# Token shift by transfers inside SBUF, and one over the sums spread by VectorE, in the transformer gate of a one-core kernel

## The reference, cut to what matters

```python
def shift_token(t):
    t1, t2 = jnp.split(t, 2, axis=-1)
    t2 = jnp.pad(t2, ((0, 0), (1, 0), (0, 0)))[:, :-1]
    return jnp.concatenate([t1, t2], axis=-1)

def _layer(x, wqkv, qs, ksc, wo, lg, lb, w1, b1, w2, b2):
    q, k, v = jnp.split(shift_token(x) @ wqkv, 3, axis=-1)   # to heads
    q, k = rotary_xpos(l2norm(q) * qs, l2norm(k) * ksc)
    o = local_attention(q, k, v)            # softmax over 64 + 64 keys
    x = x + o @ wo
    h = shift_token(x)
    mu, var = h.mean(-1, keepdims=True), h.var(-1, keepdims=True)
    h = (h - mu) / jnp.sqrt(var + 1e-05) * lg + lb
    a, g = jnp.split(h @ w1 + b1, 2, axis=-1)
    return x + (a * jax.nn.gelu(g, approximate=False)) @ w2 + b2
```

## Time and profile before

| | |
|---|---|
| median of 3 runs | 5196.27 us (5194.27 to 5201.23) |
| profiled execution, its own time | 5186.17 us |
| its span | 5184.8 us |
| busy over the span | PE 88%, DVE 61%, ACT 48%, POOL 45% |
| the gate, from the first transfer of a table to the last product | 1158.7 to some 1638 us, 9% of the span |
| steady units | 5 with 20 windows, 1257.71 to 1537.56 us: 56.0 us each |
| outside them | 12 windows of the first unit and the last two |
| one product of 128x512 on PE | two passes, 0.43 us each |
| masks and scores of one window on PE | from 1394.59 to 1396.14 us |

### The profile page before, as it was taken

One profiled execution on the slowest core, in us unless ns is written; L12 is line 12 of the kernel. 1 busy time (PEld: TensorE's weight loads), 2 busy tenths in 40 slices (PEclk: granted clock), 3 DMA queues, 4 the chain that ended last, 5 costly groups with the idle time before them and its releaser, 6 DMA issues. The chain is left out here.

```text
span 5184.8 us, 69828 instructions
## 1 busy us (share of the span) xinstructions
PE 4583.3 (88%) x27948; PEld 2248.3 (43%) x27948; DVE 3137.6 (61%) x4142; ACT 2498.2 (48%) x3813; POOL 2314.1 (45%) x1323
## 2 busy tenths in 40 slices
PE   5999999988987877877799999986799999999997
PEld 3444444445664333333322222223455555555554
DVE  4656565636665777753377777844465655565664
ACT  2344444446664455552256666661244444444443
POOL 0455555558661577780100000000066666666674
PEclk8999999989997899988889999997899999999998
DMA  0000000011110000000000000000000000000000
GB/s 32 3 3 3 3 3 3 3 36 27 32 25 12 2 2 2 1 1 23 3 2 1 2 2 1 1 1 9 10 3 3 3 1 3 3 3 1 3 1 9
DMA packets 57045, 35.95 MB, mean 7 GB/s; under 512 B 31268, under 2 KB 48976, under 8 KB 56464
## 3 DMA queue, kind: packets, MB, share of 16 engines
q1 hardware_dynamic: 56720, 31.49, 2.4%
HBM read 22.16 MB, written 1.05 MB: 4 GB/s over the span
## 5 line engine op out<-in xcount | busy, mean ns | idle before, releaser
L793 DVE TENSOR_REDUCE L_part<-banks 128x2 f32<-128x1024 f32 (+2 forms) x1600 | 1882.0, 1190 | 995.9 <-PE banks L644 856.9
L778 ACT ACTIVATE L_weights<-banks 128x1024 f32<-128x1024 f32 (+1 forms) x1600 | 1580.4, 1000 | 1055.3 <-PE banks L676 841.0
L702 PE MATMUL banks<-L_weights,L_V 128*32 128x512 f32 (+3 forms) x6400 | 1501.6, 605 | 5.8 <-ACT L_weights L778 3.7
L1000 POOL TENSOR_TENSOR L_wsum<-L_wsum,L_weights 128x1024 f32<-128x1024 f32 (+1 forms) x448 | 983.9, 2196 | 55.6 <-ACT L_weights L778 2.8
L983 POOL TENSOR_TENSOR L_wsum<-L_wsum,L_two 128x1024 f32<-128x1024 f32 x240 | 570.4, 2377 | 860.2 <-DVE L_two L967 857.8
L702 PEld LDWEIGHTS banks<-L_weights,L_V 128*64 128x64 f32 (+1 forms) x6400 | 284.7, 123 | 461.5 <-issue 398.5
L676 PE MATMUL banks<-L_QH,L_KH 64*128 64x512 f32 (+3 forms) x1664 | 432.4, 453 | 17.8 <-issue 10.2
L2502 POOL MEMSET F_xr<- 128x16 f32 x1 | 0.1, 125 | 933.8 <-POOLq L97 933.8
L644 PE MATMUL banks<-L_KH,L_QH 64*128 64x512 f32 (+3 forms) x1664 | 373.6, 430 | 30.8 <-ACT L_weights L778 17.5
L676 PE MATMUL banks<-L_QL,L_KH 64*128 64x512 f32 (+3 forms) x1664 | 372.8, 383 | 0.0
L676 PE MATMUL banks<-L_QM,L_onesrow 64*128 64x512 f32 (+3 forms) x1664 | 372.8, 381 | 0.0
(11 more groups left out here) (450 smaller groups left out, 5978.9 us busy)
## 6 DMA issues: line engine op xcount, KB each, us to landing
F_early<-F_V SPq DMA_DIRECT2D x63, 128.0 KB, 2.4
F_tab<-xpos SPq DMA_DIRECT2D x8, 512.0 KB, 4.0
F_h<-L_ffn_h_w SPq DMA_DIRECT2D x2, 1024.0 KB, 7.9
F_wqkv<-L_ffn_wqkv SPq DMA_DIRECT2D x2, 768.0 KB
L_cos<-rope_cos SPq DMA_DIRECT2D x1, 1024.0 KB, 4.9
L_sin<-rope_sin SPq DMA_DIRECT2D x1, 1024.0 KB, 6.9
out<-X SPq DMA_DIRECT2D x1, 1024.0 KB, 5.1
F_w<-L_ffn_w_w SPq DMA_DIRECT2D x3, 256.0 KB, 4.2
```

The costliest lines, as they stand in the source:

```text
L702: mm = pe.e.matmul(O[r, c:BANK], self.V[g % 2][:, kt, h, :], self.W[x % self.NW][:, y, c:BANK], start=kt < starts, stop=kt >= tiles - starts)
L778: act.e.activation(self.W[x % self.NW][:, :, c:BANK], self.banks(it)[:, :, c:BANK], ACT.Exp, scale=self.scale).then_inc(self.exped, 1)
L793: dve.e.tensor_reduce(self.part[n % 3][:, pr, j, p, :], self.banks(it)[:, :, 0:wide], AX.X, ALU.max).then_inc(self.mx_read, 1)
L1000: pool.e.tensor_tensor(acc[:, :, c:BANK], acc[:, :, c:BANK], W[:, :, c:BANK], ALU.add).then_inc(self.summed, 1)
```

## The change

- `shift`: PE's products and the constant `row_moves` are gone. DVE copies the first 64 features of x to z; SP moves the other 64 by one row inside SBUF (127 rows of 256 bytes) and, but for the first tile of a sequence, one row from the tile before. `bn_stats` becomes an item of its own, `stats`, one step later, and waits for the transfers.
- `invert`: the reciprocal reads each of the 8 sums 64 times and writes 128x512; there is one buffer of it instead of two. It moves from the odd step to the even one, behind `wturn` of its own window. `over` then is four transposes instead of 16 products.
- Ranks: `layernorm` and `lengths` go from 0 and 1 to 4, the rank of `join` and `shift`. Of one rank, in step 2, stand in this order: layernorm of unit u - 1, join and shift of unit u, lengths of unit u + 1.
- `QKV`: the queries of tile 3 stay, the values come later (steps -10, -8, -6, -4 from the unit's first instead of -12, -9, -7, -6); seven buffers V instead of eight.

```diff
-        self.mask, self.moves, self.zero = ...
+        self.mask, self.zero = ...
-    QKV = [..., (-12, 2, 1), (-12, 0, 2), (-11, 2, 0), (-10, 3, 1), (-9, 3, 0), (-9, 1, 2), (-7, 2, 2), (-6, 3, 2)]
+    QKV = [..., (-12, 2, 1), (-11, 2, 0), (-10, 3, 1), (-10, 0, 2), (-9, 3, 0), (-8, 1, 2), (-6, 2, 2), (-4, 3, 2)]
                 put(first + 2 * i + 2, ("join", u, i), ("shift", u, i))
+                put(first + 2 * i + 3, ("stats", u, i))
-        rank = {"turn": 0, "moments": 0, "layernorm": 0, "lengths": 1, "table": 3, "join": 4, ..., "shift": 9, "norm": 10, "root": 10}
+        rank = {"turn": 0, "stats": 0, "moments": 1, "table": 3, "join": 4, "shift": 4, "layernorm": 4, "lengths": 4, ..., "norm": 10, "root": 10}
-                items += exp + [("invert", w + 1)] * whole(w + 1) + [("score", w + 2)] * whole(w + 2) + rest + [("over", w), ("values", w)] * whole(w)
+                items += exp + [("score", w + 2)] * whole(w + 2) + rest + [("over", w), ("values", w)] * whole(w)
-                items += exp + turns + [("wturn", w)] * whole(w) + [it for it in rest if it not in turns]
+                items += exp + turns + [("wturn", w), ("invert", w)] * whole(w) + [it for it in rest if it not in turns]
+            elif it[0] == "shift":
+                self.shift(sp, it)
+    def shift(self, sp, it):
+        u, i = it[1:]
+        moved = self.z_moved[i % 2]
+        self.yread(sp, ("join", u, i))
+        if u >= 2:
+            self.ymade(sp, ("zturn", u - 2))
+        sp.e.dma_start(self.z[u % 2][1:P, i, 64:P], self.x[u % 2][0:P - 1, i, 64:P]).then_inc(moved, 16)
+        if u % 4 or i:
+            before = self.x[u % 2][P - 1:P, i - 1, 64:P] if i else self.x[(u + 1) % 2][P - 1:P, 3, 64:P]
+            sp.e.dma_start(self.z[u % 2][0:1, i, 64:P], before).then_inc(moved, 16)
-        for h in range(8):
-            y, j = h % 2, h // 2
-            m = pe.e.matmul(Y[64 * y:64 * y + 64, j * P:(j + 1) * P], self.rden[t % 2][:, h:h + 1].to_broadcast([P, 64]), self.core.ident[:, :], start=True, stop=True)
+        for j in range(4):
+            m = pe.e.transpose(Y[:, j * P:(j + 1) * P], self.rden[:, 2 * j:2 * j + 2, :].rearrange("p h a -> p (h a)"), self.core.ident[:, :])
-    def shift(self, pe, it):
...
-        m = pe.e.matmul(Y[:, 64:P], self.moves[:, 0, :], own[:, 64:P], start=True, stop=before is None)
-        if before is not None:
-            m = pe.e.matmul(Y[:, 64:P], self.moves[:, 1, :], before[:, 64:P], start=False, stop=True)
-                if t >= 2:
-                    self.ymade(dve, ("over", t - 2))
-                dve.e.reciprocal(self.rden[t % 2][:, :], self.den[t % 2][:, :]).then_inc(self.den_made, 1)
+                if t:
+                    self.ymade(dve, ("over", t - 1))
+                over = self.den[t % 2][:, :].rearrange("p (h a) -> p h a", a=1).to_broadcast([P, 8, 64])
+                dve.e.reciprocal(self.rden[:, :, :], over).then_inc(self.den_made, 1)
             elif kind == "shift":
                 u, i = it[1:]
-                self.ymade(dve, it)
+                self.yread(dve, ("join", u, i))
                 if u >= 2:
                     self.ymade(dve, ("zturn", u - 2))
-                dve.e.tensor_copy(self.z[u % 2][:, i, :], self.ybanked(it)[:, 0:P]).then_inc(self.y_dve, 1)
-                self.yread(dve, it)
+                if u % 4 == 0 and i == 0:
+                    self.chain.step(dve.e.memset(self.z[u % 2][0:1, i, 64:P], 0.0))
+                self.chain.step(dve.e.tensor_copy(self.z[u % 2][:, i, 0:64], self.x[u % 2][:, i, 0:64]))
+            elif kind == "stats":
+                u, i = it[1:]
+                dve.wait_ge(self.z_moved[i % 2], self.moves(u, i))
+                dve.wait_ge(self.stepped, self.chain.n)
                 self.chain.step(dve.e.bn_stats(self.st6[u % 2][:, i, :], self.z[u % 2][:, i, :]))
```

More of the change, by code:

```diff
@@ L1511 @@
     UNITS, STEPS = 8, 32
-    FREED = {"turnx": "act", "qkv": "act", "turn": "dve", "join": "dve", "shift": "dve", "zturn": "act", "gate": "act", "up": "dve", "down": "dve", "over": "act"}
-    QKV = [(-15, 0, 1), (-15, 0, 0), (-14, 1, 1), (-13, 1, 0), (-12, 2, 1), (-12, 0, 2), (-11, 2, 0), (-10, 3, 1), (-9, 3, 0), (-9, 1, 2), (-7, 2, 2), (-6, 3, 2)]
+    FREED = {"turnx": "act", "qkv": "act", "turn": "dve", "join": "dve", "zturn": "act", "gate": "act", "up": "dve", "down": "dve", "over": "act"}
+    QKV = [(-15, 0, 1), (-15, 0, 0), (-14, 1, 1), (-13, 1, 0), (-12, 2, 1), (-11, 2, 0), (-10, 3, 1), (-10, 0, 2), (-9, 3, 0), (-8, 1, 2), (-6, 2, 2), (-4, 3, 2)]
     SPINS = [(-8, 0, 0), (-7, 1, 0), (-6, 0, 1), (-5, 1, 1), (-4, 2, 0), (-3, 2, 1), (-2, 3, 0), (-1, 3, 1)]
@@ L1526, in __init__ @@
         self.b1, self.lgb, self.gains = two("b1", [P, 2, 3]), two("lgb", [P, 2]), two("gains", [P, 2, 64])
-        self.mask, self.moves, self.zero = sb("mask", [P, 2, 1, P], BF16), sb("moves", [P, 2, P]), sb("zero", [P, 1])
+        self.mask, self.zero = sb("mask", [P, 2, 1, P], BF16), sb("zero", [P, 1])
         self.hT = two("hT", [P, BANK + 1])
@@ L1533, in __init__ @@
         self.kT, self.qT = two("kT", [P, 4, 5 * P]), [sb(f"qT{i}", [P, 4, P]) for i in range(3)]
-        self.V, self.early = [sb(f"V{i}", [P, BANK]) for i in range(8)], two("early", [P, BANK])
+        self.V, self.early = [sb(f"V{i}", [P, BANK]) for i in range(7)], two("early", [P, BANK])
         self.ov = sb("ov", [P, BANK])
         self.wts, self.wT = two("wts", [P, 8, P]), two("wT", [P, 8, P])
-        self.nm, self.den, self.rden = two("nm", [P, 8]), two("den", [P, 8]), two("rden", [P, 8])
+        self.nm, self.den, self.rden = two("nm", [P, 8]), two("den", [P, 8]), sb("rden", [P, 8, 64])
         self.oT, self.x, self.z = two("oT", [P, BANK]), two("x", [P, 4, D]), two("z", [P, 4, D])
@@ L1565, in ahead @@
         load = Loads(sp.e, loaded)
-        load(self.moves[:, :, :], io["row_moves"])
         for i in range(2):
@@ L1612, in plan @@
             put(first + 14, ("down", u))
-        rank = {"turn": 0, "moments": 0, "layernorm": 0, "lengths": 1, "table": 3, "join": 4, "zturn": 4, "turnx": 5, "gate": 5, "spin": 6, "qkv": 7, "up": 8, "down": 8, "shift": 9, "norm": 10, "root": 10}
+        rank = {"turn": 0, "stats": 0, "moments": 1, "table": 3, "join": 4, "shift": 4, "layernorm": 4, "lengths": 4, "zturn": 4, "turnx": 5, "gate": 5, "spin": 6, "qkv": 7, "up": 8, "down": 8, "norm": 10, "root": 10}
         items = self.items = []
@@ L1687, in early_values, with moves @@
             sp.wait_ge(self.pv, t - 1)
-        sp.e.dma_start(early[64:P, :], self.V[t % 8][0:64, :]).then_inc(loaded, 16)
+        sp.e.dma_start(early[64:P, :], self.V[t % 7][0:64, :]).then_inc(loaded, 16)
         if t:
-            sp.e.dma_start(early[0:64, :], self.V[(t - 1) % 8][64:P, :]).then_inc(loaded, 16)
+            sp.e.dma_start(early[0:64, :], self.V[(t - 1) % 7][64:P, :]).then_inc(loaded, 16)
+    def shift(self, sp, it):
[8 more added lines that the diff above has]
+            sp.e.dma_start(self.z[u % 2][0:1, i, 64:P], before).then_inc(moved, 16)
+    def moves(self, u, i):
+        return 16 * sum(1 if v % 4 == 0 and j == 0 else 2 for v in range(u + 1) for j in range(i % 2, 4, 2) if v < u or j <= i)
     def tensor(self, pe):
@@ L1792, in values @@
         for j in range(4):
-            for x, V in enumerate((self.early[t % 2], self.V[t % 8])):
+            for x, V in enumerate((self.early[t % 2], self.V[t % 7])):
                 for y in range(2):
@@ L1805, in join @@
             m = pe.e.matmul(Y[:, 0:P], self.oT[t % 2][:, j * P:(j + 1) * P], self.wo[u // 4][:, j, :], start=j == 0, stop=j == 3)
-        m.then_inc(self.y_made, 1)
-    def shift(self, pe, it):
[L1810 to L1815, removed]
-        m = pe.e.matmul(Y[:, 64:P], self.moves[:, 0, :], own[:, 64:P], start=True, stop=before is None)
-        if before is not None:
-            m = pe.e.matmul(Y[:, 64:P], self.moves[:, 1, :], before[:, 64:P], start=False, stop=True)
         m.then_inc(self.y_made, 1)
@@ L1899, in qkv_act @@
         if x == 2:
-            if t >= 8:
-                act.wait_ge(self.pv, t - 6)
-            act.e.activation(self.V[t % 8][:, :], Y, ACT.Copy).then_inc(self.y_act, 1)
+            if t >= 7:
+                act.wait_ge(self.pv, t - 5)
+            act.e.activation(self.V[t % 7][:, :], Y, ACT.Copy).then_inc(self.y_act, 1)
             return
@@ L2050, in layernorm @@
         z = self.z[u % 2]
-        self.yread(dve, ("shift", u, 3))
         for i in range(4):
@@ L2737, in constants @@
     c["band_mask"] = bf16_bits(np.stack([nokeys, band]))
[L2738 to L2741, removed]
     even = (np.arange(D) // 2 * 2).astype(np.float32)
```

8 lines of the change are left out of this document (3 added, 5 removed).

## The result

The changed kernel took 5247.72 us (median of 6 runs, 5238.82 to 5253.15) beside 5197.45 us of the kernel before (6 runs, 5194.27 to 5202.69): ratio 1.0093, 95% interval 1.008 to 1.0106. It is slower by 50 us, where the forecast was 22 us. The time lies inside the range, and the reciprocal, its place on the path and the places of the new stalls are as forecast. The size is not: of the 7.0 us that a steady unit loses, 4.7 arise in steps 2 to 5, for which I had summed 0.5.

What follows compares the result with a forecast made beforehand. PE's products and, in steps 2 and 3, DVE's order bound the unit. Five steady units 8.5, 12 windows 11, tail 1.4, copy of z 2, minus 0.4: 22.5 us more, 5218 us; range 5172 to 5262.

Steps and rivals of the forecast that it cites:

- The reciprocal: On DVE, 128x512 takes 3.4 us, 3.2 us more a window; DVE becomes busy 47.6 us a unit.
- rival of a cheap reciprocal: 512 elements cost 0.69 us on DVE, a unit gains 5.9 us, 5155 us; chance 0.21 together with a milder form, 5175.
- Its place: The reciprocal stands in the even step between the copy of the weights and the sum of x.
- Steps 2 and 3: Sum of x 1.2 us later, lengths ends at 1381.8, keys turned at 1386.9 against 1386.98: nothing gained.
- Steps 4 and 5: Third gate product waits some 2.2 us for x, scores still end before the maximum: no loss, no gain.
- Steps 6 and 7: Down waits for a sum of x 3.1 us late; after savings on PE the window ends 1.2 us late.
- The clock: Rival: new stalls in steps 4, 6 and 0 grow past 3.16 us and halve PE's clock; 42 us more, 5260; chance 0.07.
- The transfer: The 127 rows land in 2.4 us; rival: one engine carries them, 3.8 us, 0.9 us more a unit, 5224, chance 0.15.
- PE's saving: Shift's products 0.62 us and over 0.43 less: 1.05 us a window, 4.2 a unit; PE's work 45.8 us.
- Outside the steady units: 12 windows of the first and last two units add 0.9 us each, 11 us; the tail adds some 1.4.

Runs made afterwards that it cites:

- e5: Changed kernel with the reciprocal of 8 sums and a DVE copy spreading them to 512, four transposes kept: 5176.12 us, ratio 0.9959.
- e4: Changed kernel with the same wide reciprocal placed behind layernorm, sum of x, copy of z and lengths: 5178.83 us, ratio 0.9963.
- e12: Kernel before with the changed order, shift on PE, 8 reciprocals spread by DVE copy, four transposes, and join and shift ahead of layernorm: 5174.42 us, ratio 0.9950.
- e10: Kernel before with only the values' new places and seven buffers V: 5191.06 us, ratio 0.9980.
- e9: Changed kernel with 14 unread identity products on PE ahead of down's wait for a bank: 5248.82 us, ratio 1.0092.
- e3: Changed kernel with the move of 127 rows cut into two transfers of 112 and 15 rows: 5248.01 us, ratio 1.0095.
- e8: Kernel before with the narrow reciprocal in its new place, new ranks, values' order and seven buffers V; shift on PE: 5175.91 us, ratio 0.9955.

## Why the prediction was right in sign and half the size

**The reciprocal: right.** 3.4 us from two rows of another width, 3342 ns measured; DVE 47.6 us a unit, 46.56 measured. The rival of a cheap reciprocal fell with it. e5 shows that the rival also had its gain too high: with the spread at 0.78 us a unit is 2.7 us shorter than before (53.2 instead of 55.97), not 5.9.

**Its place: right, and stronger than I had it.** The reciprocal lies between the weights' copy and the sum of x in every window. e4 moves it and wins 69 us with its length unchanged.

**Steps 2 and 3: right as a chain.** Lengths end 9.1 us after the copy starts (predicted 9.4), and the turn of keys follows 14.46 us after the copy (predicted 1386.9 - 1372.42 = 14.5). Two sizes are off. The product into oT starts 1390.78 - 1387.69 = 3.09 us after its turn of keys. In the trace of before it is 1370.61 - 1369.00 = 1.61:

```profile
1369.00 0.66 PE L1746 MATMUL banks<-ident,F_kn 128*128 128x128 f32 x4
...
1370.61 0.69 DVE L1951 TENSOR_TENSOR F_oT<-banks,F_ov 128x512 f32<-128x512 f32 x1 [2.02 <-ACT F_ov L1852]
```

That is 1.5 us where I had 0.5. And the unit that I read the earlier trace rows was the longest of five: its stretch was 17.98 us, the mean is 17.23. A chain set by DVE and POOL takes 19.4 us in every unit, so against the mean the loss is 0.75 us more.

**Steps 4 and 5, "no loss, no gain": the step that failed.** Three things were left out: the half clock behind the turn of keys, ACT's order, and the place of the values' product. The turn of keys waits for POOL 2.20 us here (4.70, 3.11, 4.70 and 3.24 in the other four units), and behind it the clock falls in all five. Stretches of the changed kernel, then DVE, PE and ACT of the same window:

```profile
1408.00:1410.00 2.00, 2.00 (x13) 2.00 (x11) 1.25 (x3) 0.00 (x0) 2.00 (x3) 0.52 0.00 0
1410.00:1412.00 2.00, 2.00 (x9) 1.74 (x9) 2.00 (x2) 0.00 (x0) 1.89 (x2) 0.62 0.00 0
```

```profile
1409.75 1.23 DVE L1938 COPY F_wT<-banks 128x1024 f32<-128x1024 f32 x1 [0.75 <-PE banks L1788]
...
1414.43 1.09 PE L1742 MATMUL banks<-F_zT,F_w 128*85 128x512 f32 x2 [1.19 <-DVE F_x L1969]
...
1417.28 0.60 ACT L1909 ACTIVATE F_sq<-banks 128x512 f32<-128x512 f32 x1 [0.26 <-PE banks L1729]
...
1422.58 1.09 PE L1742 MATMUL banks<-F_zT,F_w 128*85 128x512 f32 x2 [1.10 <-ACT F_qn L1912]
```

*The clock.* The weights are turned at half clock, so their copy starts 2.70 us after the turn of keys instead of 2.00, and with it the reciprocal and the sum of x. In the five units it starts 3.68, 3.57, 2.70, 3.68 and 3.43 us after the turn, and the two steps take 19.07, 18.96, 18.09, 19.07 and 18.82: each time 15.39 us from the copy on. So what the copy is late, the unit is longer. That is 3.41 - 2.00 = 1.4 us of the 2.55 in the mean, near the 1.65 that e12's two kinds of unit differ by. The unit shown is the mildest.

*ACT's order and the values' place.* The other 1.1 us: the third gate product waits for x, the keys' product stands behind it and behind that of the values on PE, and its square on ACT comes 10.2 us after the turn instead of 6.3. The exponents and the queries' square are queued behind that square; F_qn ends 15.5 us after the turn instead of 12.1, and up's third product waits for its bank. I had checked only that the scores end before the maximum. Of the later square 0.9 us, and of the unit some 0.3, are the values' order, as e10 shows; the rest is read from the traces and was not tried alone.

**Steps 6 and 7: the mechanism right, 1.2 us predicted, 2.62 measured.** Down waits for x, as said. Where the clock stayed at 1.00, in the fifth unit, the steps take 13.60 - 12.28 = 1.32 us more than before, as predicted. In the other four down takes 4.12 to 4.57 us instead of 2.84, and they take 1.6 us more again.

**The clock: a rival at 0.07 that came true in two of its three places.** It had some 2 us for each; the traces give 1.4 in steps 4 and 5 and 1.3 in steps 6 and 7: 2.7 us a unit, half of the 5.3 that I missed. Its condition, a stall that grows past 3.16 us, does not part the cases. At the turn of keys three of the five stalls were longer, two were not, and the clock fell in all; at down all were 2.11 us, and it fell in four of five. The error was to take a shorter stall for safe because one of 3.16 us had left the clock at 1.00. e9 won back only 0.07 us of a unit, since its products ended too late.

**The transfer: its rival came true.** The 127 rows go over one engine; stats waits 2.0 us a unit, 2.2 predicted for this case, and the product into oT is 1.0 us later than the forecast had it, 0.9 in the rival. No run took that wait away alone; e3 sped up the data and didn't shorten the sum of the waits.

**PE's saving: smaller, and worth nothing.** PE is busy 1.2 us less in a unit (48.79 to 49.99), 4.2 predicted; products at half clock are longer and take part of it. e8 shows it from the other side: with the shift on PE the unit is shorter.

**Outside the steady units.** 11 us predicted for the 12 windows and 1.4 for the tail, some 19 measured.

Together: the traces show 54 us where I had 22. Of these 32, 5 x 5.3 = 26 are in the steady units: 13.5 of them the half clock, 8 the two sizes of steps 2 and 3, the rest ACT's order and the values' place, less what steps 0 and 1 won. Some 7 are outside them. The time lies inside the range only because the range goes up to the clock's case, to which I gave 0.07.

## What to carry to other kernels

Where two engines' work is ordered by hand, a long operation costs by what stands behind it on its own engine: the same 3.34 us reciprocal cost 67 us in front of the sum that PE waits for, and about nothing two to four items later. When a wait is moved to another place on PE, follow what is queued behind it through the next engine's own order, here ACT's square ahead of its exponents, and take the lengths of stretches as means over all like units, not from the one on the screen. Give the half clock a price at every new stall of PE, also a short one: here it was half of what the forecast of a unit missed, and like units of one trace, with and without it, gave that price without a run of its own. An engine's saved work shows only when no other engine's chain sets the unit; here POOL, started by lengths on DVE, sets it next.

## What the runs showed of the hardware that I had not expected

- The granted clock of PE fell to 0.50 and 0.52 after stalls of 2.11 and 2.20 us, while after the stall of 3.16 us in the earlier trace rows it was 1.00. The length of one stall doesn't tell which level follows: of five stalls of 2.11 us in the changed kernel four were followed by the half clock, of five of 2.75 us in e12 three. With products in place of the 2.11 us it stayed at 1.00.
- The same four tensor_scalar of 128x128 took 1.11 us with POOL idle and 4.38 beside POOL's tensor_tensor.
- 127 rows of 256 bytes between SBUF and SBUF ran at a flat 18 GB/s; as 112 + 15 rows they ran at 111 to 169 GB/s, and were ready no sooner in the mean.
- The copy of 128x64 within SBUF, put at 0.3 us, took between 0.12 and 0.97 us, 0.39 in the mean. The reciprocal of 128x512 took 3342 ns, 4.8 times as long as a product of the same shape (692).
